# Preparing the next graph ahead of the lookups' pace, and two lookup units moved, in a 16-graph GNN kernel on one core

## The reference

```python
# layer 0, for each graph
rank = cumsum(neigh) - neigh; nb = neigh.sum(-1)
skip = where(nb > T, ceil(nb / K), 1)                 # T, K = 10, 2
rem = neigh & (skip > 1) & (rank % skip == skip - 1) & mask
adj_d = where(rem | rem.T, 0, adj_)                   # neighbours that are left
s = sort(where(adj_d > 0, x, inf), axis=neighbours); nv = adj_d.sum(2)
agg = sum over tau in (.25, .5, .75) of w * interpolate(s, tau * (nv - 1))   # per node and channel
x = layernorm(x + mask * (relu((x + agg) @ W1 + b1) @ W2 + b2))
# layer 1: relu(D^-1/2 (A + I) D^-1/2 (x @ kernel)), layernorm; then two more layers
```

## Time and profile before

| | |
|---|---|
| median of 3 runs | 3188.49 us (3183.55 to 3193.70) |
| profiled execution | 3183.33 us, its span 3181.5 us |
| busy share of the span | DVE 88%, PE 70%, ACT 62%, PEld 32% |
| mean granted TensorE clock | 0.818 of full speed |

### The profile page before, as it was taken

How to read it: one execution, slowest core, us unless ns; L and a number is a source line. 1 busy time by engine, 2 the same in 40 slices (tenths; PEclk the granted TensorE clock), 3 DMA queues, 4 the chain that set the end, 5 groups by cost and what they waited for, 6 DMA issues and landing times.

```text
span 3181.5 us, 45583 instructions
## 1 busy us (share of the span) xinstructions
PE 2234.6 (70%) x16081; PEld 1004.7 (32%) x16234; DVE 2805.6 (88%) x5398; ACT 1987.2 (62%) x3077; POOL 12.4 (0%) x24
## 2 busy tenths in 40 slices
PE   0000014387888888898888888888898889776996
PEld 0000002232333333333333333333333333225664
DVE  7999998999989999999999999999999999546776
ACT  2111443178887878787788787778788777741322
POOL 0000000000000000000000000000000000000000
PEclk6555557688989989898999989899999989886777
DMA  3001000000101001010100101010100100000101
GB/s 68 0 0 26 31 0 0 22 15 20 38 7 35 12 29 26 17 33 12 36 11 31 21 21 34 11 38 8 34 13 29 34 10 19 10 20 27 40 26 40
DMA packets 126916, 72.05 MB, mean 23 GB/s; under 512 B 95513, under 2 KB 110059, under 8 KB 126699
## 3 DMA queue, kind: packets, MB, share of 16 engines
q1 hardware_dynamic: 122570, 68.23, 8.4%
q10 hardware_dynamic: 4128, 1.05, 0.2%
HBM read 41.05 MB, written 15.58 MB: 18 GB/s over the span
## 4 chain that ended last, share of the span: by engine, by line
DVE 57%; PE 27%; ACT 8%; issue 6%; SPq 1%; DMA 1%; DVEq 0%; ACTq 0%
PE ring L624 5%; DVE picked L1527 5%; PE rows L665 4%; ACT hot L1078 3%; PE found_bank L677 3%; PE bcast L637 3%; DVE picked L1519 3%; DVE picked L1511 3%; DVE picked L1521 3%; DVE picked L1493 3%; DVE keys L1329 3%; DVE keys L1330 3%; PE bank L919 2%; DVE picked L1499 2%; DVE delta L1370 2%
## 5 line engine op out<-in xcount | busy, mean ns | idle before, releaser
L1078 ACT ACTIVATE hot<-bcast,consts 128x1024 f16<-128x1024 f32 x744 | 831.5, 1118 | 112.8 <-PE bcast L637 112.8
L624 PE MATMUL ring<-member,neigh_t 128*128 128x512 bf16 x1925 | 495.4, 396 | 40.8 <-issue 16.0
L665 PE MATMUL rows<-hot,table 128*64 128x512 f16 x3072 | 515.8, 416 | 0.0
L1071 ACT ACTIVATE prod<-rows 128x512 f32<-128x512 f32 x720 | 432.1, 600 | 10.1 <-PE rows L665 10.1
L637 PE MATMUL bcast<-idx_t,consts 32*128 32x512 f16 x1488 | 309.5, 413 | 169.4 <-ACT hot L1078 167.6
L654 PE MATMUL rows<-fine_rows,consts 32*128 32x512 bf16 x768 | 314.2, 409 | 18.1 <-DMA fine_rows<-turned 18.0
L624 PEld LDWEIGHTS ring<-member,neigh_t 128*128 128x128 bf16 x2048 | 189.3, 102 | 325.0 <-issue 110.0
L562 PE MATMUL ring<-identb,adj_b 128*128 128x128 bf16 x256 | 33.2, 294 | 358.7 <-ACT adj_b L974 347.3
L677 PE MATMUL found_bank<-prod,consts 128*32 128x512 f32 x1536 | 233.1, 683 | 11.2 <-ACT prod L1071 10.4
L637 PEld LDWEIGHTS bcast<-idx_t,consts 32*128 32x128 f16 x1488 | 70.6, 92 | 510.7 <-ACT hot L1078 338.0
L1527 DVE TENSOR_TENSOR picked<-picked 128x3072 uint16<-128x3072 uint16 (+2 forms) x192 | 209.5, 1091 | 11.2
(11 more groups left out here) (347 smaller groups left out, 4324.7 us busy)
## 6 DMA issues: line engine op xcount, KB each, us to landing
late<-in_adj_dram SPq DMA_DIRECT2D x16, 1024.0 KB, 5.4
adjt_d<-neigh_t SPq DMA_DIRECT2D x16, 512.0 KB, 2.7
fine_rows<-turned SPq DMA_DIRECT2D x512, 8.0 KB
fine_rows<-turned SPq DMA_DIRECT2D x512, 16.0 KB
turned<-adjt_d SPq DMA_DIRECT2D x16, 512.0 KB, 3.6
adj_s<-adjt_d SPq DMA_DIRECT2D x16, 512.0 KB, 4.0
xt_d<-keys SPq DMA_DIRECT2D x2, 1024.0 KB, 10.4
parts_d<-parts SPq DMA_DIRECT2D x4, 512.0 KB, 6.9
```

The lines of the kernel that those rows point to most:

```text
L624: ins = mm(ring[u % 2][:, :], kept_t[:, j, P * i:P * i + P], member[:, j, n // 2, 512 * (n % 2):512 * (n % 2) + 512], start=(j == 0), stop ...
L665: ins = mm(rows[u % 2][C * h:C * h + C, :], table[:, s, GROUPS * h + g8, :], hot[:, u % HOT, h, :], start=False, stop=(s == 1), skip_group ...
L1071: run(prod[:, u % DEEP, :], rows[u % 2][:, :], ACT.Relu).then_inc(S["prod_by_act"], 1)
L1078: run(hot[:, u % HOT].rearrange(flat), spread_bank(l, u)[0][:, 0:2, :].rearrange(flat), ACT.Relu, bias=eq_bias[:, :]).then_inc(S["hot_read ...
```

## The change

- **Order on DVE.** `region` becomes `ahead`, and DVE's order has no units in it. The helpers are generators now: `beside(ins, other)` issues an instruction of the bits' chain, then one instruction of `other`, and only then waits for the former. `ranks`, `ffn_end`, `gcn_start`, `middles`, `gcn_middle` with `drops`, `members` and `limits` stand between the instructions of the chain so. The second `pop` now stands behind `clear_own`, and `limits` inside `bits_next`.
- **Tags in the sum.** DVE no longer multiplies `first` with a tag for each group (L1508, four times a graph); `sum_first` multiplies with `tagged`, 15 scaled identities, in place of `identb`.
- **A fence in `count_up`.** One more matmul of 512 columns for each tile adds 4096 where there is an edge, so `drop` is one comparison (`tensor_scalar`) without the product with `adj_b`.
- **Units.** `LEAD` goes from (0, 4, 9, 14, 22) to (0, 5, 10, 15, 24): two units of the region move into the first and the fourth tile. The parts of PE's and ACT's region stand between other units.
- **The end.** `last_region` and `behind` replace the two last regions: the dense layers of graph 14 begin after 2 units of the last graph's lookups, not after 22.

```diff
-LEAD = (0, 4, 9, 14, 22)
+LEAD = (0, 5, 10, 15, 24)
 LATE = LEAD[NT]
-STEP = [LATE + n for n in (0, 1, 2, 4, 6, 7, 9, 11, 13, 14, 15, 17, 19, 21)]
...
+                mm(ring[i % 2][:, :], fence[:, :], adj_b[:, i, :], start=True, stop=False)
                 for j in range(NT):
-                    ins = mm(ring[i % 2][:, P * j:N], neigh_t[:, j, P * i:P * i + P], upper[:, 0:N - P * j], start=(j == 0), stop=(j == NT - 1))
+                    ins = mm(ring[i % 2][:, P * j:N], neigh_t[:, j, P * i:P * i + P], upper[:, 0:N - P * j], start=False, stop=(j == NT - 1))
...
-                    ins = mm(first_sum.rearrange("p (k c) -> p k c", k=TAUS), identb[:, :], plane[:, :, C * g:C * g + C], start=(g == 0), stop=(g == G - 2),
+                    ins = mm(first_sum.rearrange("p (k c) -> p k c", k=TAUS), tagged[:, g, :], plane[:, :, C * g:C * g + C], start=(g == 0), stop=(g == G - 2),
...
-                units(l, STEP[13])
+                units(l, LATE + 16)
                 if p is not None:
                     pe.wait_ge(S["member_ready"], NT * p + NT)
                     chunk(p, 0, 0)
                     pe.wait_ge(S["nv_read"], p + 1)
                     chunk(p, 0, 1)
                 for n in range(2, CW, 2):
-                    units(l, STEP[13] + n // 2)
+                    units(l, LATE + 16 + n)
...
+            def last_region(l, d):
+
+                units(l, 2)
+                dense_first(d)
+                units(l, 6)
+                dense_second(d)
+                units(l, 16)
+                dense_turn(d)
...
+            def beside(ins, other):
+
+                n = did(ins)
+                next(other, None)
+                need(n)
...
             def drop(b, i):
 
                 dve.wait_ge(S["apart_ready"], NT * b + i + 1)
-                stt(out=drop1[:, i, :], in0=apart_of[:, i % 2, :], scalar=s2[:, i:i + 1], in1=adj_b[:, i, :], op0=ALU.is_equal, op1=ALU.mult).then_inc(S["drop_ready"], 1)
+                ts(drop1[:, i, :], apart_of[:, i % 2, :], s2[:, i:i + 1], None, ALU.is_equal).then_inc(S["drop_ready"], 1)
...
-                tt(first_at[:, 0:last], first[:, C:], first_tag[:, 1:, :].rearrange(flat), ALU.mult).then_inc(S["tile_read"], 1)
-                dve.wait_ge(S["tile_read"], NT * b + i + 1)
-                need(count[0])
-                tt(starts[:, :, 0:last], starts[:, :, 0:last], first_at[:, 0:last].unsqueeze(1).to_broadcast([P, TAUS, last]), ALU.mult).then_inc(S["first_picked"], 1)
+                tt(starts[:, :, 0:last], starts[:, :, 0:last], first[:, C:].unsqueeze(1).to_broadcast([P, TAUS, last]), ALU.mult).then_inc(S["first_picked"], 1)
...
+            def ahead(t_of, p, d):
+
+                ranks = chain(rank_bits(p), members(p, 0)) if p is not None else nothing
+                ffn = chain(degree(d), ffn_end(d)) if d is not None else nothing
...
+                bits_start(t_of, ranks)
+                pop(wl, x2, x4, x8, t, ranks)
+                alone(ranks)
+                bits_first(ffn)
+                alone(ffn)
+                start = chain(pause(2), gcn_start(d)) if d is not None else nothing
                 if p is not None:
                     clear_own(p)
...
+                pop(wl, x2, x4, x8, t, start)
+                alone(start)
+                middle = middles(p) if p is not None else nothing
+                bits_second(middle)
+                alone(middle)
...
+                other = chain(pause(2), limits(p)) if p is not None else nothing
+                ending = chain(gcn_end(d), pause(2), gcn_done(d)) if d is not None else nothing
+                other = chain(other, ending)
+                bits_next(t_of, other)
+                tell("idx_ready")
+                alone(other)
+                restart()
```

More of the change, by code:

```diff
@@ L8 @@
 from contextlib import ExitStack
+from itertools import chain
 import concourse.bass as bass
@@ L1180, in region @@
                         chunk(p, 0, n + 1)
+                    if n == 4 and d is not None:
+                        root_of(d, 2)
                 units(l, UNITS + 2)
@@ L1270, in then, with alone, pause @@
                 need(did(ins))
+            def beside(ins, other):
+                n = did(ins)
+                next(other, None)
+                need(n)
+            def alone(other):
+                for _ in other:
+                    pass
+            def pause(n):
+                for _ in range(n):
+                    yield
+            nothing = iter(())
             def restart():
@@ L1387, in replay @@
                     if e == 33:
-                        limits(0)
+                        alone(limits(0))
                 tell("rank_ready")
@@ L1588, in bits_first @@
                 did(tt(mixed, wl, wh, ALU.bitwise_xor))
-                units(l, STEP[3])
-                did(ts(step, bit, 0.0, None, ALU.is_equal))
-                then(tt(r, r, t, ALU.subtract))
-                then(ts(t.bitcast(I16), bit, -1.0, None, ALU.mult))
-                did(tt(a_of, blk, bit, ALU.add))
+                beside(ts(t, t, 31, None, ALU.bitwise_and), other)
+                beside(tt(bit, r, t, ALU.is_ge), other)
+                beside(tt(t, t, bit, ALU.mult), other)
@@ L1594, in bits_first @@
+                stays = did(ts(step, bit, 0.0, None, ALU.is_equal))
+                beside(tt(r, r, t, ALU.subtract), other)
+                flags = did(ts(t.bitcast(I16), bit, -1.0, None, ALU.mult))
+                a_made = did(tt(a_of, blk, bit, ALU.add))
+                need(stays)
                 did(tt(upper_half, wh, step, ALU.mult))
-                then(tt(t, t, mixed, ALU.bitwise_and))
-                then(tt(wl, wl, t, ALU.bitwise_xor))
+                need(flags)
+                beside(tt(t, t, mixed, ALU.bitwise_and), other)
@@ L1721, in region @@
[L1721 to L1739 removed]
+                yield from norm_b(xb(l))
@@ new lines, in drops @@
+            def drops(b, lo, hi):
+                for i in range(lo, hi):
+                    drop(b, i)
+                    yield
+            def ahead(t_of, p, d):
+                ranks = chain(rank_bits(p), members(p, 0)) if p is not None else nothing
+                ffn = chain(degree(d), ffn_end(d)) if d is not None else nothing
+                need(count[0])
+                dve.wait_ge(S["sums_ev"], 2 * (NT * t_of + NT))
+                bits_start(t_of, ranks)
[4 more added lines that the diff above has]
+                start = chain(pause(2), gcn_start(d)) if d is not None else nothing
@@ L1740, in region @@
                 if p is not None:
                     clear_own(p)
-                units(l, STEP[5])
-                if d is not None:
-                    gcn_start(d)
+                pop(wl, x2, x4, x8, t, start)
[3 more added lines that the diff above has]
+                alone(middle)
                 if p is not None:
-                    middles(p)
+                    alone(members(p, 1))
+                other = gcn_middle(d) if d is not None else nothing
@@ L1763, in region @@
-                units(l, STEP[9])
-                if t_of is not None:
-                    narrow(x4, 4)
-                units(l, STEP[10])
+                    other = chain(other, drops(p, 0, 2))
+                narrow(x4, 4, other)
+                alone(other)
+                other = drops(p, 2, NT) if p is not None else nothing
+                narrow(x2, 2, other)
+                alone(other)
+                other = members(p, 2) if p is not None else nothing
+                bits_last(other)
```

558 lines of the change are left out of this document (313 added, 245 removed).

## The result

The changed kernel takes 3312.57 us (median of 4 runs, 3308.57 to 3315.64) against 3186.14 (also 4 runs) for the kernel before: ratio 1.0392, 95% interval 1.037 to 1.0414. It is slower, as forecast, but by 126 us and not by 25. The profiled execution has a span of 3306.8 us.

A forecast was written before the change was run, and what follows sets the result against it. No engine alone bounds: a loop DVE clear_own, PE counts, DVE limits and nv_read, PE chunks and units does. 3183.33 + 21 (periods) - 9 (graph 0) + 0.5 - 0.7 - 1 + 16.5 (end) = 3211 us; range 3140 to 3242.

The forecast's parts named there:

- end term: Last graph's lookups: PE idles behind unit 2 for x_t, so units and totals come later; +16.5 us (13 to 18).
- the saving in the tiles is swallowed: DVE at tile 1: 11 us ahead, it waits longer there for PE's products, so its savings are lost.
- Rival B: Whole kernel: DVE bounds throughout, every us saved counts, -11 x 13, about 3045 us; chance 0.07.
- Case D: Counted as slower, chance 0.08, most of it left out of the range; its claim isn't in the text given.
- the main one: Whole kernel: slower, 3211 us, its own range 3195 to 3235; chance 0.45.
- P + 121.9 + 20.9 = P+142.8: Next period's start on PE, counted from period start P: 142.8 against 141.1; +1.6 taken for 13 periods, +21 us.
- store landed: Store ahead of clear_own: lands at P+88.4 (P is the period's start), against P+84.8 before, after dense_first at P+72.8.
- `clear_own` done to `nv_read`: DVE's way between these: 32.8 us (31 to 34.5) against 30.7 before, with about 2.5 of waits covered.
- from there to L737: PE from chunk(0,1) to the next period: 20.9 us against 15.1, for three more units and one total.
- Graph 1: Graph 1's period: +0.5 us; it and its like were said to have slack on DVE.
- Rival A: Full periods: chain shorter than counted, DVE always early, PE and ACT alone set 138.3 a period, 3156 us; chance 0.25.
- rival C: Whole kernel: nothing moves much; at -1 a period the 13 give back the end's cost, 3190 us; chance 0.15.

The follow-up runs named there:

- the added instruction: Changed kernel with one more DVE tensor_tensor of 960 columns in each tile, its result unused: 3314.82 us.
- the old places: Changed kernel with LEAD, STEP and PE's and ACT's region as before: 3272.15 us; with ACT's third root_of also behind the first chunks, 3163.12 us, 138.7 a period.
- the three edits: Changed kernel with four buffers for apart_of, the second pop ahead of clear_own, and x_t of graph 14 early: 3202.48 us, ratio 1.0044 to the kernel before.
- the pair of runs around ACT's third root: Changed kernel with LEAD, STEP and PE's and ACT's region as before, third root_of among the next graph's first chunks, 3272.15 us, or behind them, 3163.12 us.

## Why the prediction was right and wrong

**The sign and the end were right.** The end term was 16.5, measured 19.9; taking its cause away gave 29.3, since the early dense layers bring 9 once free. The first L737 came 12.7 earlier, forecast 10. The drop takes 0.35 with 0.27 to the next start (forecast 0.29), where the three-operand instruction took 0.75 for the same 512 columns. That the saving in the tiles is swallowed held to 2 us (the added instruction).

**Rival B**, that DVE bounds throughout, fell: DVE's busy share went from 88% to 80% and the time rose by 3.9%. Even with the old places DVE's new order brought 2.4 a period, not the 11 that this rival counts. DVE's work, the largest busy share of all, did not give the time here; the table of waits had ruled it out beforehand.

**Case D** of the chances, slower yet than the main one, has a size that no run shows. In its place the runs showed 3312.57 us, above the 3242 at which the range ends, with the granted clock at half of full speed for 27.3 us a period where it was 24.7.

**The step that failed: "The next period begins at P + 121.9 + 20.9 = P+142.8 ... I take 1.6".** Measured is 149.3, an error of 6.5 a period, 85 of the 101 us that were missing. By its own terms:

| term | forecast | measured |
|---|---|---|
| store landed | P+88.4 | P+91.3 |
| `clear_own` done to `nv_read` | 32.8 | 35.1 |
| from there to L737 | 20.9 | 22.1 |

The first: `dense_first` came at P+74.6, not P+72.8, and the store 1.1 later again. I gave the two units 2.55; measured are 4.9, of it 3.7 busy and 0.9 of waits for `hot`. I had priced their work at full clock. A unit's L667 takes 1.07 for four where the granted clock is recorded at half of full speed, and 0.63 where it is recorded at full; from the period's start to `dense_first` such stretches grew from 6.8 to 10.2 us, in the whole period from 24.7 to 27.3 (means over nine periods). PE after, in the period shown:

```profile
1480.30 0.63 PE L667 MATMUL rows<-hot,table 128*64 128x512 f16 x4
...
1489.76 1.07 PE L667 MATMUL rows<-hot,table 128*64 128x512 f16 x4
```

The second is smaller, 2.3, but holds the mistake in the mechanism, which I could have seen in the orders. The sum for DVE's way counted DVE's instructions and let its waits for ACT and PE be "now covered by that work". They weren't: DVE waits 1.4 for ACT's fourth `apart` and 1.4 for the count (13.0 and 12.3 in nine periods). Behind both stands ACT's wait for the first drop, which appears nowhere in the prediction. I had the order of DVE (drop 4 later) and the order of ACT (third `apart` three units sooner) and compared neither with the two buffers between them. With four buffers 37 us come back and this term measures 32.0; with the pop in the store's wait it is 55 us and 32.1. Either brings the term back to its forecast of 32.8. The wait for the store was itself forecast, and the pop's place in it was not tried in thought.

The third was near. The waits of lone units behind the first chunks (0.81 above, the model's was 0.65) came as counted.

**Graph 1** was given +0.5 and took 10.5: the same places and orders hold there, and I had treated its slack on DVE as cover. With `LEAD` as before its period is 139.6, with the pop early 140.1, against 144.2.

**Rival A**, 138.3 a period if PE's waits for DVE vanish, never came about for the changed kernel: even with the three edits it stays at 143.35, with 3.9 of waits for DVE left. Nor is it a floor for the other places: they run at 138.7, and at 136.6 with the same edits. The 6.8 between these two are, on PE, waits for `hot` (12.2 against 10.4 a period), waits for DVE (3.9 against none) and 0.8 more of busy time. Which of the moved parts in the region brings them wasn't separated, except that it isn't the two units in the tiles (143.15 without them).

**Sums.** Rival A's terms add up to 138.1 and not 138.3, and with the sum's other terms its time is about 3151; rival C's is about 3177, not 3190. The main sum holds as added. Neither slip touches the step above.

## What to carry to other kernels

When an engine's order changes, list for every buffer with two slots who frees it and who asks next, with the new times of both; a saving on the engine with the most work doesn't help where that engine then reaches the freeing instruction later (here 145 us less of DVE's work, but its first drop 16.0 us behind `clear_own` and not 12.2, and ACT waiting 3.7 a period for it). Put work that nobody waits for into the wait that is already there (here the second `pop` in the wait for the store) before moving work of other engines. And test a change of two orders as four corners: here DVE's order alone gained 2.4 us a period and the places alone cost 4.5, and 6.1 more came only from the pair.

## What was not expected of the hardware

Idle on PE came with more than its own length. In the pair of runs around ACT's third root a wait of 4.3 us a period went together with 4.1 us more of busy time for the same matmuls (granted clock 0.90 against 0.92), and with 9 us a period more at half of full speed. That the wait brings the lower clock is the author's reading; no run separates the two.
